# Ten stored maps instead of sixteen, sparse resize taps, attention output with channels on partitions, and one row addition on VectorE instead of GpSimd

## What is computed

```
kv_sel = vmap(lambda t, i: t[i])(kv_pix, idx)        # 4 windows of 64 keys for each window
att = softmax(einsum('bpqhd,bpkhd->bphqk', q_pix * SCALE, k_sel))
o = einsum('bphqk,bpkhd->bpqhd', att, v_sel)         # 4 heads of 32 channels
xh = xh + (unwin(o) + depthwise5x5(v)) @ wo_w + wo_b
xh = xh + gelu(layernorm(xh) @ mlp_w1 + mlp_b1) @ mlp_w2 + mlp_b2
```

## Time and profile before

| | |
|---|---|
| median of 3 runs | 14038.39 us |
| the profiled execution | 14078.87 us, its span 14077.1 us |
| mean granted TensorE clock | 0.919 |
| PE busy | 11000.8 us (78%) |
| ACT busy | 9084.8 us (65%) |
| DVE busy | 8501.4 us (60%) |
| POOL busy | 6883.1 us (49%) |

### The profile page before, as it was taken

The page is one execution under the profiler, slowest core; times in us unless marked ns, Lnnn a source line. Parts: engine busy times, 40 slices in busy tenths (PEclk is TensorE's granted clock), DMA queues, the critical chain, the costliest instruction groups (busy, mean ns, idle before and its releaser), DMA issues.

```text
span 14077.1 us, 469161 instructions
## 1 busy us (share of the span) xinstructions
PE 11000.8 (78%) x170988; PEld 8551.4 (61%) x170988; DVE 8501.4 (60%) x12547; ACT 9084.8 (65%) x20318; POOL 6883.1 (49%) x6167
## 2 busy tenths in 40 slices
PE   3568888888888888888888888888888888851887
PEld 2346666666666666666666666666666666631666
DVE  7445756666665757666675666666575666631743
ACT  1226776766676776767676676667677676741677
POOL 0005464545545454545545454554545454466467
PEclk8669999999999999999999999999999999975999
DMA  4214454544444444444444454444445444431444
GB/s 138 72 41 114 111 123 107 122 109 117 113 116 114 110 120 111 116 111 119 112 111 118 110 123 106 120 112 117 113 109 120 110 119 111 118 78 25 106 126 115
DMA packets 1848261, 1535.10 MB, mean 109 GB/s; under 512 B 1006880, under 2 KB 1382176, under 8 KB 1841760
## 3 DMA queue, kind: packets, MB, share of 16 engines
q1 hardware_dynamic: 1835776, 1494.30, 42.3%
q0 software_dynamic: 9216, 2.38, 0.2%
HBM read 1297.70 MB, written 198.21 MB: 106 GB/s over the span
## 4 chain that ended last, share of the span: by engine, by line
PE 38%; issue 15%; ACT 13%; DVEq 10%; DVE 9%; SPq 6%; POOL 4%; POOLq 3%; DMA 2%; ACTq 1%
PE bank_small L930 8%; PE windows L960 6%; DVEq L1441 6%; PE bank_small L981 6%; PE bank_scores L852 5%; ACT hats L1171 3%; DVE ol L1442 3%; ACT hats L1175 2%; DVEq L1422 2%; PE bank_scores L869 2%; POOL gbuf L710 2%; SPq L492 2%; PE bank_post L903 2%; POOLq L639 2%; PE bank_turned L973 1%
## 5 line engine op out<-in xcount | busy, mean ns | idle before, releaser
L1497 DVE TENSOR_TENSOR prod<-windows,wy 128x640 f32<-128x640 f32 x4032 | 3293.4, 820 | 1927.1 <-PE windows L960 1803.6
L960 PEld LDWEIGHTS windows<-fx,hats 64*64 64x64 f32 x129024 | 2652.3, 139 | 1391.6 <-issue 1322.9
L960 PE MATMUL windows<-fx,hats 64*64 64x80 f32 x129024 | 3283.9, 243 | 240.8 <-issue 201.6
L638 POOL TENSOR_TENSOR prod<-prod 128x768 f32<-128x768 f32 x1344 | 2467.9, 1836 | 1503.5 <-DVE prod L1497 1496.4
L1171 ACT ACTIVATE hats<-hats,cst 128x512 f32<-128x512 f32 x4032 | 2877.1, 714 | 162.2 <-DMA hats<-sample_columns 101.5
L1442 DVE SCALAR_TENSOR_TENSOR ol<-xpad,lepw,ol 128x448 f32<-128x448 f32 x2688 | 2464.0, 917 | 236.1 <-issue 1.8
L1175 ACT ACTIVATE hats<-hats 128x512 f32<-128x512 f32 x4032 | 2513.8, 623 | 6.7
L930 PE MATMUL bank_small<-wom,ofp 128*128 128x216 f32 x8064 | 1625.1, 357 | 63.2 <-issue 63.2
L640 POOL TENSOR_TENSOR prod<-prod 128x384 f32<-128x384 f32 x1344 | 1557.4, 1159 | 217.7 <-issue 30.7
L643 POOL TENSOR_TENSOR val<-prod 128x384 f32<-128x384 f32 x1344 | 1502.5, 1118 | 241.2 <-issue 156.0
L852 PE MATMUL bank_scores<-ksel,qbd 128*128 128x256 f32 x3136 | 989.2, 443 | 723.9 <-DVE osb L1427 588.4
(11 more groups left out here) (191 smaller groups left out, 13515.9 us busy)
## 6 DMA issues: line engine op xcount, KB each, us to landing
hats<-sample_columns SPq DMA_DIRECT2D x2688, 336.0 KB
ksel<-k_windows SPq DMA_DIRECT2D x3136, 32.0 KB
vsel<-v_windows SPq DMA_DIRECT2D x3136, 32.0 KB
fx<-map_columns SPq DMA_DIRECT2D x64, 420.0 KB
xpad<-in_x SPq DMA_DIRECT2D x17, 1568.0 KB, 11.8
map_columns<-fst SPq DMA_DIRECT2D x16, 1624.0 KB
feat_up<-fdense SPq DMA_DIRECT2D x16, 1568.0 KB, 14.2
q_windows<-qb SPq DMA_DIRECT2D x112, 224.0 KB, 2.5
```

Source lines behind the costliest of these rows:

```text
L638: pool.tensor_tensor(v[:, :, 0:n], v[:, :, 0:n], v[:, :, n:2 * n], ALU.add)
L960: last[h] = pe.matmul(o[m], hat[:, m], fx[XP * h:XP * h + XP, g, row:row + WR, :].rearrange("p r c -> p (r c)"), start=True, stop=True)
L1497: dve.tensor_tensor(o, x, w.unsqueeze(3).to_broadcast([128, 2, CP * WR, CG]), ALU.mult).then_inc(s_wm, 1)
```

## The change

1. **Ten maps.** `MAP_OF` gives the map of each image, `NMAP` is 10, and the loops of the setup run over `NMAP`. SP's main loop of 14 iterations is split into three (2 iterations with map 0, 9 with map i-3, 3 with map 9), so that the address can be worked out from the loop's counter. The other engines keep one loop.
2. **Sparse taps.** Taps 1 and 2 are one product each over the whole image; taps 0 and 3 are products and additions over an eighth or a seventh of it.
3. **Attention output.** `pv` computes for each head 32 channels x 64 queries, with the values as the stationary operand, and once more with a block of ones, which gives the row sums on the same partitions. There are 16 products instead of 4. The `fold` products and `osb` are gone; `exps` has no `accum_out`; `scale_heads` is a reciprocal over 64 elements and one product into `ob`.
4. **Row addition.** The first of the three additions of `add_rows` is done by DVE (`add_pairs`), after `maxes` in every third slot.

```
 def pv(i, w):
     pe.wait_ge(s_pt, cnt(i, P2, w + 1))
-    for h in range(2):
-        for m in range(2):
-            mm = pe.matmul(bs[:, h * W2:(h + 1) * W2], pt[:, h, m, :],
-                           vsel[w % NKV][:, m, h * W2:(h + 1) * W2], start=(m == 0), stop=(m == 1))
-    mm.then_inc(s_pv, 1)
+    hold(pe, "pe")
+    last = [None] * HEADS
+    for part in range(2):
+        for m in range(2):
+            for hd in range(HEADS):
+                r = slice(hd * HD, (hd + 1) * HD)
+                v = vsel[w % NKV][:, m, r] if part == 0 else const("ones")
+                last[hd] = pe.matmul(bs[r, part * W2:(part + 1) * W2], v,
+                                     pt[:, hd // 2, m, (hd % 2) * W2:(hd % 2 + 1) * W2],
+                                     start=(m == 0), stop=(m == 1))
+    for hd in range(HEADS):
+        last[hd].then_inc(s_pv, 1)
 def post(i, b, k):                      # PE
-    if k == 0:
-        pe.wait_ge(s_os, cnt(i, P2, (b + 1) * NWIN))
...
-        for j in range(NWIN):
-            mm = pe.matmul(bp[:, j * W2:(j + 1) * W2], osb[(b * NWIN + j) % NOSB][:], const("fold"),
-                           start=True, stop=True)
-        mm.then_inc(s_po, 1)
 def scale_heads(i, w):                  # DVE
-    dve.reciprocal(rinv[:], sm[w % 2][:])
-    dve.drain()
-    for g in range(2):
...
-        last = dve.tensor_tensor(o, x, rinv[r, :].unsqueeze(2).to_broadcast([64, 2, HD]), ALU.mult)
-    last.then_inc(s_os, 1)
+    dve.wait_ge(s_pv, cnt(i, HEADS * P2, HEADS * (w + 1)))
+    dve.reciprocal(rinv[:], bs[:, W2:2 * W2])
+    dve.drain()
+    dve.tensor_tensor(ob[(w // NWIN) % 2][:, (w % NWIN) * W2:(w % NWIN + 1) * W2], bs[:, 0:W2], rinv[:],
+                      ALU.mult).then_inc(s_os, 1)
 def add_rows(i, t, g):                  # POOL
-    pool.wait_ge(s_wm, cnt(i, NT * Q, t * Q + CPG * (g + 1)))
-    pool.tensor_tensor(v[:, :, 0:n], v[:, :, 0:n], v[:, :, n:2 * n], ALU.add)
-    pool.drain()
+    pool.wait_ge(s_ra, cnt(i, NG * NT, NG * t + g + 1))
     pool.tensor_tensor(v[:, :, 0], v[:, :, 0], v[:, :, 1], ALU.add)
+def add_pairs(i, t, g):                 # DVE
+    v = prod[(t * NG + g) % 2]
+    n = WR // 2
+    dve.drain()
+    dve.tensor_tensor(v[:, :, 0:n], v[:, :, 0:n], v[:, :, n:2 * n], ALU.add).then_inc(s_ra, 1)
```

More of the change, by code:

```diff
@@ L78, in const_layout @@
     at = 0
-    for name, n in (("ident", 128), ("fold", 64), ("mean", 128), ("centre", 128), ("posadd", 3 * S), ("kyrow", S),
+    for name, n in (("ident", 128), ("ones", HD), ("mean", 128), ("centre", 128), ("posadd", 3 * S), ("kyrow", S),
                     ("gidx", S), ("ibase", B), ("rows", WR), ("xneg", 1), ("mid", 1), ("valid", 1), ("eps", 1),
@@ L96, in resize_matrix @@
     return (w / w.sum(0, keepdims=True)).astype(np.float32)
+WBAT = resize_matrix(2, B).T
+MAP_OF = [0] * B
+for _n in range(1, B):
+    MAP_OF[_n] = MAP_OF[_n - 1] + int(not np.array_equal(WBAT[_n], WBAT[_n - 1]))
+NMAP = MAP_OF[NIMG - 1] + 1
+FIRST = [MAP_OF.index(m) for m in range(NMAP)]
+NCONST = const_layout()
 def constants():
@@ L110, in constants @@
     put("ident", np.eye(128))
-    put("fold", np.concatenate([np.eye(64), np.eye(64)], 0))
+    put("ones", 1.0)
     put("mean", 1.0 / C)
@@ L217, in build @@
         nmx = [sb(f"nmx{s}", [128, 2]) for s in range(2)]
[L218 to L220 removed]
+        rinv = sb("rinv", [128, W2])
+        ob = [sb(f"ob{s}", [128, BAND]) for s in range(2)]
         hid = sb("hid", [128, HID, BAND])
@@ L603, in _ @@
             body(1, 0)
-            with sp.Fori(2, NIMG) as i:
-                body((i, 0), (i, -1))
+            lo = 2
+            while lo < NIMG:
+                same = MAP_OF[lo] == MAP_OF[lo - 1]
+                hi = lo + 1
+                while hi < NIMG and (MAP_OF[hi] == MAP_OF[hi - 1]) == same:
+                    hi += 1
+                with sp.Fori(lo, hi) as i:
+                    body((i, 0), (i, -1), [MAP_OF[lo]] if same else MAP_OF[lo] - lo)
+                lo = hi
             body(None, NIMG - 1)
@@ L777, in _ @@
             pe.wait_ge(s_src, 64)
-            for n in range(NIMG):
+            for n in range(NMAP):
                 map_turns(n)
@@ L1325, in _ @@
+                for n, r in enumerate((0, 6)):
+                    o = up.rearrange("p y (q r) -> p y q r", r=7)[:, :, :, r]
+                    dve.tensor_tensor(o, o, pe_[:, n], ALU.add)
+                dve.drain()
             wbat = const("wbat")
@@ L1347, in _ @@
             map_image(0)
-            for n in range(NIMG):
-                if n + 1 < NIMG:
+            for n in range(NMAP):
+                if n + 1 < NMAP:
                     map_image(n + 1)
@@ L1361, in _ @@
             dve.memset(hats[:], 0.0)
-            for s in range(NOSB):
-                dve.memset(osb[s][:], 0.0)
             dve.tensor_scalar(posw[:, 4:5], posw[:, 4:5], 1.0, None, ALU.add)
@@ L1529, in body @@
                             maxes(xi, w)
+                        if di is not None and q % CPG == CPG - 1:
+                            add_pairs(di, t, q // CPG)
                         if fi is not None and q == PXT + 1:
```

124 lines of the change are left out of this document (67 added, 57 removed).

## The result

The changed kernel takes 14284.78 us, the median of 4 runs (14273.17 to 14314.87), beside 14040.53 us of the kernel before on the same chip: a ratio of 1.0175, with a 95% interval from 1.0158 to 1.0192. It is slower. The forecast was 13928 us and faster, and 14284.78 lies outside its range of 13710 to 14210. The profiled execution has a span of 14277.0 us, 199.9 more than before.

A forecast was written before the change was run, and what follows sets the result against it. The prediction saw mixed limits: in a middle body's later stage 14 windows limited by PE, 20 by DVE, some 8 by neither. Setup -152, fifteen middle bodies +117 (+7.8 each), first -45, last -30: -110 from 14038.4, 13928 us, range 13710 to 14210.

The forecast's parts named there:

- Setup, -152: Setup: a shorter resize (-57 us) and six maps fewer (-93 us) save 152 us, between 140 and 155.
- `pv` -0.35 in 14 PE-limited windows: Attention windows of a middle body: the new `pv` occupies PE 0.59 us instead of 0.94, saving 14 x 0.35 = 5 us.
- `fold` -8: Attention of a middle body: removing the fourteen `fold` passes per band saves 8 us per image.
- sums -2: Attention of a middle body: two accumulator reads leave ScalarE, saving 2 us per image at the MLP's windows.
- `scale_heads` +0.10: Attention windows: `scale_heads` takes 0.79 us instead of 0.69, +0.10 us per window, from -0.18 to +0.39.
- Rivals A and B: A: 0.79 us reciprocal, VectorE limits attention, 14149 us, chance 0.19. B: `pv` pieces don't overlap, about 14310, chance 0.08.
- Row addition: Attention windows: the addition on DVE costs 1.05 us per group; relief of the taps returns 0.29 us per window.
- 8 by neither: Later windows of a middle body: some 8 are limited by neither PE nor DVE, leaving DVE some 3 us idle each.
- The sign that was named: Light attention windows: growth from 8.2 us to about 9 was expected; growth over 1 us would prove the forecast wrong.
- First 27 slots +4.5: First 27 slots of a middle body: nine additions cost 9.5 us, relief of the taps returns 5, together +4.5 us.
- Last body -30: Last body: moving L638 off POOL saves 30 us, between 10 and 50, with PE the next limit.
- rival B: Attention: the new `pv`'s pieces don't overlap, +1.05 us in PE-limited windows, about 14310 us in all, chance 0.08.

The follow-up runs named there:

- e3: The kernel before with only the setup changed (ten maps, sparse taps, SyncE's loop split in three): 13762.77 us, ratio 0.9799.
- e6: e3 with the 336 transposes of the six missing maps still issued on TensorE, into banks nobody reads: 13881.28 us, ratio 0.9881 to the kernel before.
- e1: The changed kernel with the row addition back on GpSimd: 13887.93 us, ratio 0.9879 to the kernel before.
- e11: e1 with the division left out (reciprocal over one column instead of 64, result unused): 13798.97 us, ratio 0.9801 to the kernel before.
- e2: The kernel before with only the row addition moved to VectorE: 14564.94 us, ratio 1.0362.
- e4: The changed kernel with the row addition on VectorE placed behind the taps of its slot instead of ahead: 13973.15 us, ratio 0.9938 to the kernel before.
- e12: e3 with the load of the next x four slots later, in slot 214: 13752.74 us, ratio 0.9774 to the kernel before.
- e9: e1 with the load of the next x in slot 214 instead of 210: 13821.97 us, ratio 0.9816 to the kernel before.
- e14: e3 with two of pv's four products cut to one column instead of 64: 13839.92 us, ratio 0.9851 to the kernel before.

## Why the prediction was wrong

- **Setup, -152: right.** The resize ended at 80.76 and the weights were issued at 248.35 instead of 397.67, 149 us earlier.
- **Not in the sum at all: TensorE's stop after the loop's edge.** It went with the six maps' transposes: 147 us of e3's 296, and e6 brings 118 back. The changed kernel has this gain too, by luck; without it the forecast would have been further off.
- **`pv` -0.35 in 14 PE-limited windows, `fold` -8, sums -2: a step that failed, in its limit.** The sizes were right (0.58 us occupied against 0.59 forecast), the limit was not. I took windows with PE busy 10.25 of 10.9 us for windows in which TensorE ends last everywhere. Between `pv` and `scores` VectorE does. Of -238 us for the new output (first body included) there came +125 where the addition stays on GpSimd: 66 to 88 from the x load that lands ahead of GpSimd's jump in e1, about 45 from `scale_heads` (0.86 us instead of 0.69, an estimate at the price that e11 measured for 0.39), and nothing from `pv` and `fold` but 25 in the first body (its end at 909.8 in e1, 934.9 in e3), which the middle bodies gave back. Beside the moved addition the x load costs nothing, and the new output comes to some +16 by the estimate above: still no gain where -238 stood.
- **`scale_heads` +0.10: right within its bounds.** It is +0.17: 0.55 us for the reciprocal, which the prediction's two bounds enclose, and which is less than the 0.69 of its other estimate. Rivals A and B, at their own conditions, did not happen: the reciprocal isn't 0.79, and the pieces overlap.
- **Row addition: the other step that failed, in the windows that pay.** I had it cost 0.76 us (+1.05, -0.29 of relief) in 20 windows of a body and nothing in the others. In e2, alone, it costs 0.76 us in all 27 windows without products, so the slack of the "8 by neither" wasn't there, and 0.62 in each of the 13 heavy ones, which I took to hide it: 30.6 us in the 41 windows of a body where I had 15. The relief did not come either. Two taps that lay under GpSimd's additions for 2.51 us before lie under them for 2.83 now. I had named this ("at worst nothing does, as L640 and L643 slide under the taps") and priced it as a relief of nothing. In e4's place the relief came, and more than forecast: the taps' mean went to 0.733 where 0.83 had been the hope.
- **The sign that was named** (a light window growing by over 1 us) came in the window shown, with 1.6 us; the mean over the 27 windows without products is 0.83, near the forecast's 0.86. The miss lies more in the heavy windows: +0.61 us where -0.35 was forecast.
- **First 27 slots +4.5:** +2.1 (means of ten bodies: 83.4 in e1, 85.5 in the changed kernel). **Last body -30:** -9.7; TensorE, busy 414 of 510.8 us, and "issue" took over.
- The middle bodies were forecast at +7.8 us and came at +26.2.

The time of 14285 us is near rival B's 14310, by another cause. Of versions that compute everything, e3, ten maps and sparse taps alone, is the fastest with e12: 2% faster than the kernel before.

## What to carry to other kernels

When work is moved between VectorE and GpSimd, write down which instruction on the one runs beside which on the other after the move, not only how much; an addition behind the taps cost 100 us, ahead of them 400 to 500. When parts are run alone, add them in a second order too: e1 had a cost of its own, some 7 us per body, that neither end of the change has. A high busy share says little about a link: before counting a gain, ask what ends last between this instruction and the one that waits for it. And check by one run each whether a gain comes with code that moved: dead instructions ahead of a loop changed this kernel by 118 us.

## What the runs showed of the hardware

- TensorE can stop for 3 to 5 us within like products after a hardware loop's edge (4.55 us before, 3.12 in e6), and whether it does depends on how many instructions stand ahead of the loop (e3, e6).
- After GpSimd's jump over a long unused block the next instruction came 4.46 us later in e9 and 4.33 in the changed kernel, and 8.22 us later in e1, where a load of 1568 KB was issued 2.5 us ahead of the jump. SyncE's longest issue just behind that load took 6.8 to 8.8 us in each of the ten traces read with the load in slot 210, and 1.2 at most in e9 and e12, with slot 214.
- Two taps, 1.44 us alone, took 2.83 beside two additions on GpSimd of 2.21 us, while a product with an operand in PSUM stayed at 0.82.
- A reciprocal took 0.16 us over one column and 0.55 over 64, 6.2 ns for each further element, where a product takes some 1 ns.
- Thirty-two passes of 64 columns with 32-column weights that share all rows occupied 0.58 us.
- Halving a product on TensorE made the kernel 77 us slower (e14), at a lower granted clock: 0.956 against 0.982 in the 41 windows.
